# The border to the four-head attention: seven products made twice and 25 unit-matrix products ahead of the turned maxima

## The reference

```python
xn = _layernorm(x)
s = _L1_attn_ref(xn, W_qkv, W_out)                  # 16 heads, chunks of 64 rows
g = _silu(_L1_ffn_ref(xn, ...))                     # four-head attention, then experts
x = x + s * g
```

```python
nx = _rmsnorm(X, g1)
Q = (nx @ Wq.T).reshape(B, S, H, dk).transpose(0, 2, 1, 3)   # H = 4, dk = 32
Kc = nx @ Wkc.T
Vc = nx @ Wvc.T
scores = jnp.einsum('bhsd,btd->bhst', Q, Kc) * scale
attn = jax.nn.softmax(scores, axis=-1)
out = jnp.einsum('bhst,btd->bhsd', attn, Vc)
```

## Time and profile before

| | |
|---|---|
| median of 3 runs | 646.14 us |
| lowest, highest | 642.94 us, 647.99 us |
| the profiled execution, its own time | 644.59 us |
| span from first to last instruction | 642.5 us |
| mean granted clock of TensorE | 0.987 |

### The profile page before, as it was taken

The page is one execution under the profiler, slowest core; times in us unless marked ns, Lnnn a source line. Parts: engine busy times, 40 slices in busy tenths (PEclk is TensorE's granted clock), DMA queues, the critical chain, the costliest instruction groups (busy, mean ns, idle before and its releaser), DMA issues.

```text
span 642.5 us, 12628 instructions
## 1 busy us (share of the span) xinstructions
PE 594.6 (93%) x4528; PEld 400.6 (62%) x4529; DVE 485.3 (76%) x1140; ACT 351.0 (55%) x710; POOL 358.2 (56%) x377
## 2 busy tenths in 40 slices
PE   4888899899989899969999999999999999999996
PEld 2566799667755566545555554555455543788885
DVE  5767345349968778898777787878887875798986
ACT  2645555336855456625777775767576665442222
POOL 6607400176647443607777778887787778415220
PEclk9999999999999999989999999999999998999998
DMA  9801122120000000000000000000000000000101
GB/s 294 347 2 50 51 66 65 41 55 6 0 2 2 2 3 3 3 1 1 1 1 1 1 2 1 2 0 2 1 2 1 1 2 1 1 2 1 34 0 34
DMA packets 16616, 17.33 MB, mean 27 GB/s; under 512 B 1712, under 2 KB 15024, under 8 KB 16176
## 3 DMA queue, kind: packets, MB, share of 16 engines
q1 hardware_dynamic: 15536, 14.49, 6.7%
q0 software_dynamic: 1024, 2.10, 1.1%
HBM read 11.34 MB, written 5.24 MB: 26 GB/s over the span
## 4 chain that ended last, share of the span: by engine, by line
PE 73%; DVE 12%; POOL 6%; issue 3%; ACT 3%; DMA 2%; SPq 0%; DVEq 0%; ACTq 0%; POOLq 0%
PE ps L2060 13%; PE ps L2050 10%; PE ps L2040 8%; PE ps L2188 5%; PE ps L1863 3%; DVE region L1092 3%; PE ps L1770 3%; PE ps L1753 3%; PE ps L2178 2%; PE ps L2180 2%; PE ps L2179 2%; POOL slots_in L626 2%; PE ps L1853 2%; PE ps L1951 2%; PE ps L1967 1%
## 5 line engine op out<-in xcount | busy, mean ns | idle before, releaser
L1092 DVE TENSOR_REDUCE region<-ps 128x1 f32<-128x512 f32 x256 | 160.7, 682 | 38.6 <-PE ps L2040 38.1
L1543 ACT ACTIVATE region<-ps 128x512 f32<-128x512 f32 x256 | 138.2, 600 | 58.7 <-PE ps L2050 58.7
L773 POOL TENSOR_TENSOR region<-region 128x512 f32<-128x512 f32 x80 | 108.9, 1364 | 42.2 <-ACT region L1543 38.5
L2050 PE MATMUL ps<-qmr,kr 98*128 98x512 f32 x256 | 111.9, 441 | 1.8 <-ACT region L1543 1.0
L2040 PE MATMUL ps<-kr,qmr 96*128 96x512 f32 x256 | 102.7, 411 | 2.2 <-DVE region L1092 1.5
L2060 PE MATMUL ps<-region 128*32 128x512 f32 x512 | 93.3, 609 | 0.0
L2067 PE MATMUL ps<-region,ones 128*32 128x512 f32 x192 | 93.1, 607 | 0.2 <-DVE region L1109 0.2
L778 POOL TENSOR_TENSOR region<-region 128x512 f32<-128x512 f32 x64 | 82.0, 1281 | 12.3 <-ACT region L1543 8.6
L2050 PEld LDWEIGHTS ps<-qmr,kr 98*128 98x128 f32 x256 | 48.8, 192 | 54.0 <-issue 28.8
L2040 PEld LDWEIGHTS ps<-kr,qmr 96*128 96x128 f32 x256 | 49.2, 193 | 15.5 <-DVE region L1092 9.0
L1647 ACT ACTIVATE region<-ps 128x512 f32<-128x512 f32 x36 | 21.6, 599 | 56.8 <-PE ps L2180 56.8
(11 more groups left out here) (283 smaller groups left out, 1196.6 us busy)
## 6 DMA issues: line engine op xcount, KB each, us to landing
region<-in_w SPq DMA_DIRECT2D x2, 2048.0 KB, 12.8
slots_in<-zeros SPq DMA_DIRECT2D x1, 1536.0 KB, 9.0
region<-slots_in SPq DMA_DIRECT2D x6, 256.0 KB, 2.8
slots_out<-og SPq DMA_DIRECT2D x6, 256.0 KB, 2.4
e<-in_e SPq DMA_DIRECT2D x1, 1152.0 KB, 15.4
x<-in_x SPq DMA_DIRECT2D x4, 256.0 KB, 3.6
out<-y SPq DMA_DIRECT2D x3, 256.0 KB, 2.3
e<-in_e SPq DMA_DIRECT2D x1, 576.0 KB, 17.5
```

Source lines behind the costliest of these rows:

```text
L773: ins = pool.tensor_tensor(o, held(tiles[0]), held(tiles[1]), ALU.add)
L1092: dve.tensor_reduce(mxp[:, u // HM, u % HM:u % HM + 1], bank(b), AX.X, ALU.max).then_inc(mx_read, 1)
L1543: act.activation(pm[:, t // 2, t % 2 * HM * P:(t % 2 + 1) * HM * P], bank(SCORE_BANKS[n % 3]), ACT.Exp, scale=SCM).then_inc(p_whole, 1)
L2050: pe.matmul(bank(SCORE_BANKS[n % 3]), kr[0:M_ROWS, t * P:(t + 1) * P], qr[0:M_ROWS, parity, :], start=True, stop=True).then_inc(st_filled, 1)
```

## The change

Two things are added to PE's list, and one wait is moved.

- The products of the first maxima from `u = 9` to `u = 15`, seven in number, are each issued twice in a row, into the same bank with the same operands. The semaphore that lets DVE read the bank is raised by the second.
- After the end of `chunk_order`, PE waits for `pT_ready` and then issues 25 products of `ident` with `ident`, 128x128 float32, into the first 128 columns of bank 2. Nothing reads them; the first score product overwrites the bank. They are plain products, not transposes. `turn_maxima(0, 0)` follows behind them.
- The wait for `pT_ready` therefore stands ahead of `turn_maxima`, no longer behind it.

No instruction is removed, and the other engines' lists stay as they were.

```diff
--- before.py
+++ after.py
@@ -56,6 +56,8 @@
 MU = HM * T // 512
 MAX_BANKS = (0, 1, 5)
 SCORE_BANKS = (2, 3, 4)
+UNITS_BORDER = 25
+TWICE_FROM = 9
 FIRST_BANKS = (1, 4, 5, 6, 7)
 FIRST_MAXIMA = (range(0, 5), range(5, 9), range(9, 16))
 HALVES_TILE = 1
@@ -2037,8 +2039,10 @@
                     pe.wait_ge(mx_read, i * MU + u - 2)
                 elif not first and MAX_BANKS[(i * MU + u) % 3] == 0:
                     pe.wait_ge(n_ready, NT // 2)
-                pe.matmul(bank(FIRST_BANKS[u % 5] if first else MAX_BANKS[(i * MU + u) % 3]), qm[0:R_ROWS, parity, h * P:(h + 1) * P], kr[0:R_ROWS, c:c + 512],
-                          start=True, stop=True).then_inc(mx_filled, 1)
+                o = bank(FIRST_BANKS[u % 5] if first else MAX_BANKS[(i * MU + u) % 3])
+                for _ in range(2 if first and u >= TWICE_FROM else 1):
+                    ins = pe.matmul(o, qm[0:R_ROWS, parity, h * P:(h + 1) * P], kr[0:R_ROWS, c:c + 512], start=True, stop=True)
+                ins.then_inc(mx_filled, 1)
 
             def scores_t(i, t, parity, first):
 
@@ -2098,8 +2102,10 @@
             for stage, i in chunk_order:
                 if stage in steps:
                     steps[stage](i)
+            pe.wait_ge(pT_ready, NT)
+            for _ in range(UNITS_BORDER):
+                pe.matmul(bank(2)[:, 0:P], ident[:, :], ident[:, :], start=True, stop=True)
             turn_maxima(0, 0)
-            pe.wait_ge(pT_ready, NT)
             pe.wait_ge(mx_read, MU)
 
             def project_rows(g):
```

## The result

| | before | changed |
|---|---|---|
| median | 645.51 us (8 runs) | 651.04 us (8 runs) |
| lowest, highest | 642.94, 647.99 us | 649.32, 651.76 us |
| profiled execution, its own time | 644.59 us | 651.64 us |
| its span | 642.5 us | 649.5 us |

The change makes the kernel slower: the ratio is 1.0078, with a 95% interval of 1.0057 to 1.0100, 5.5 us at the medians. Forecast were 645.2 us and a range up to 648.7.

The account below looks back on a forecast made before the run. The prediction took PE as the engine to look at, its border handover running at half clock as the cost. Terms -0.24 + 0.50 + 0.46 + 0.22 = 0.94 us less gave 646.14 - 0.94 = 645.2 us, range 642.4 to 648.7.

Parts of the forecast that it names:

- The step that failed: Before the turned maxima: 25 unit products at 0.111 us take 2.78 us, end at 284.55, delay 0.24 us.
- the sign itself: At the border: the prediction would be wrong if the 25 unit products end well after 284.55.
- The bound given beside it: At the border: at 0.235 us each the 25 unit products take 5.9 us, delaying the turned maxima 3.3 us.
- The sum's last term, -0.22: Next eight reductions of tile 1, after the handover: 4.82 us at full clock against 5.04, gain 0.22 us.
- Rival 2: After the border: clock falls a little later, five slots at 1.28 instead of 1.20 us cost 0.4; 645.8 us; 13%.
- The doubled products are covered: Ahead of the border: seven doubled products cost nothing, covered by DVE's queue of reductions; margin 0.27 us at the first.
- The moved wait: Ahead of the unit products: PE's wait for ACT's last copy, ending at 277.40, four microseconds before PE arrives, costs nothing.
- The handover at full clock: Turned maxima to first reduction of tile 1: four transposes gain 0.50 us, first score to first reduction 0.46.
- The clock is full over the border: PE, busy without a gap from 278.48 to the turned maxima, keeps granted clock 1.00 from 278 to 294.
- rival 1: At the border: clock falls all the same at the same place, only the 0.24 us delay is left; 646.4 us; 15%.
- Rival 3: From 278.5 to 284: added products meet a half clock, turned maxima 5.7 us later, 651.9 us; 6%.
- The call for a change within 1%: Whole kernel: within 1% (6.5 us) 94%, faster by over 1% 3%, slower 3%.

Follow-up runs that it names:

- the filling: In query tile 0's first seven slots the second maxima product is made twice; ratio to the kernel before 1.0047 added to the change, 0.9978 with 12 unit products.
- units_12: The change with 12 unit-matrix products in place of 25, doubled products kept; ratio 1.0017 to the kernel before.
- double_only: The change without the 25 unit-matrix products, the seven doubled products kept; ratio 0.9981 to the kernel before.

## Why the prediction was wrong

**The step that failed** is "The nearest row is eight plain 128x128 float32 products in 0.89 us at full clock, 0.111 us each". The row L2109 x8 is right and the division too, but it counts instructions of the array. The code beside it (`project_rows`) writes four products per group, in four groups, so 16 written products and 32 rows in the trace. A plain product with float32 operands is two instructions here; a transpose, or a product of float32r operands like the maxima, is one. The number 25 came from the program's list, where such a product is one row, and the duration from the trace, where it is half a product. The term should have read 25 x 2 x 0.112 = 5.6 us, end 287.37 instead of 284.55, and +3.06 us instead of +0.24. Measured: +3.08 in the profile, and 0.225 us a product between 25 and 50. The prediction had named the sign itself, that the 25 end well after 284.55: they end at 288.61, in a profile that reaches the border 1.05 us later. The bound given beside it, 3.3 us of delay, was near the truth and was set aside with "shape and type are the same". With this term alone right, the same sum gives -0.94 + 2.82 = +1.9 us.

**The sum's last term, -0.22, failed too**, and this is the rest of the way to 5. Rival 2 named the mechanism, that the clock holds over the border and falls a little later, but priced it as five slots at 1.28 instead of 1.20 us. It took the half clock to end with the stretch that DVE bounds. In all six profiles in which unit products or transposes stood at the border and nothing was filled (the change's two and four variants'), it fell 5.9 to 8.4 us behind that reduction and lasted beyond the stretch's end, into work that PE bounds. First reduction to second turned maxima took 14.3 to 15.4 us there, and 12.3 to 12.6 in the profiles where the half clock lay early or not at all (leaving out those with the filling at half clock). The early half clock of the kernel before costs 1 us at the handover; the late one, with the pause of the next paragraph, costs 1.9 to 3.1 (14.26 to 15.39 us against 12.33 with the filling). Removing the first alone is a loss.

**A part of that term is not the clock's.** L1133, a DVE instruction with two inputs in SBUF, took 1.29 us of the chain after, and 0.47 us in the same place before, where its line is L1131; it stands under the last heading. From the chain before:

```profile
292.45 0.47 DVE region L1131
```

PE was idle for 1.4 us behind it. The instruction lasted 1.36 to 1.39 us in all six of these profiles, and 0.28 to 0.29 us with 12 or 25 unit products and the filling, so those runs removed both the sparse slots and this pause. The chain of units_12, against that with the filling above, shows how much is the pause's:

```profile
314.85 1.28 DVE region L1133
...
316.78 0.50 PE ps L2044
```

PE takes the chain over 6.81 us after the first reduction (309.97) without the filling, and 5.73 us (309.77 to 315.50) with it. So of the 2.2 us between these two profiles 1.1 are the pause, and the other 1.1 are left for the half clock. For the change the same count gives 1.1 us of pause and 2.0 us of half clock. The prediction had no term for the pause. Which of the two, the sparse slots or the pause, makes the clock fall, no run here separates: in the first profile of the change and in that of the transposes the clock fell while PE was idle behind L1133, in the other four up to 1.5 us after PE had begun again.

**What was right.** The doubled products are covered (9.65 us; double_only). The moved wait costs nothing (double_only has it, at 0.9981). The handover at full clock gives back 0.98 us against 0.96 forecast. The clock is full over the border, so rival 1 did not come. Rival 3, the slower one, had the consequence, unit products that outlast DVE, and the doubled duration of 0.22 us apiece, but by the wrong cause: not a half clock but a second instruction. The call for a change within 1% (94%) came true at 0.8%, by luck: it was worked out for a gain of 0.94 us, and what came was a loss of 5.5.

## What to carry to other kernels

Count the instructions of a written product in the trace before multiplying by a duration: find the loop that writes them, and compare its count with the row's. Work that is to bridge an idle of an engine must end before what it bridges; here each written product too many costs its full 0.22 us. And ask of a dip of the clock not only what it costs where it is, but where it goes: where another engine sets the pace a half clock is cheap, and a cure that moves it into PE's own stretch must fill that stretch as well.

## What the runs showed of the hardware

- A plain 128x128 product of float32 operands is two array instructions, 0.112 us each at full clock (`x50` for 25, `x24` for 12); a float32 transpose is one (`x25` for 25, 0.109 us each), and so is a product of float32r operands (`x14` for 14).
- A DVE instruction that reads two tensors from SBUF took longer when POOL was at work, until POOL's addition had ended. The durations of L1133 in the changed kernel (ns, least, median, most):

```profile
L1133 DVE TENSOR_TENSOR region<-region x16: 279/398/1414, 255.9 to 507.6; 128x128 fp32r<-128x128 f32 x16
```

Five times as long at the most as at the least, for one shape. In the timeline above the long one starts at 295.36, when POOL's addition started at 295.31, and ends at 296.73, 0.15 us after that addition ends at 296.58. The Trainium skill ("GPSIMD Engine Reference", section "Specifications", the row on SBUF interfaces) says that these are shared with VectorE and that instructions with two SBUF inputs contend; this row agrees. Two inputs are not needed for it, though. L1103 is a CAST with one input:

```profile
L1103 DVE CAST region<-region x16: 170/534/1159, 284.9 to 528.9; 128x4 fp32r<-128x4 f32 x16
...
302.85 1.27 POOL L780 TENSOR_TENSOR region<-region 128x512 f32<-128x512 f32 x1
...
302.98 1.16 DVE L1103 CAST region<-region 128x4 fp32r<-128x4 f32 x1
```

It ends at 304.14, 0.03 us after POOL's addition, and so did the other nine of the 16 that took 0.53 us or more. L1101, a reduction with one input in SBUF, kept its 0.17 us in all 14 cases in which it started during such an addition.
- The same program took 25 us longer ahead of the border on chip 3 than on the first chip (299.0 and 274.0 us to the first reduction of the first maxima), and from there on as long (367.9 and 368.5 us).
